# The shift by the row maximum of four attention heads, in one pass of 32-row strips ahead of the scores

## The chip, the cores and the metric

The kernel runs on one core of a Trainium2 chip. The metric is device time in microseconds (us) of one execution, the median of several runs. TensorE does the matrix products into the eight banks of PSUM, ScalarE (ACT) the exponentials and copies, VectorE (DVE) the maxima and normalisation, GpSimd (POOL) small vector work, SyncE (SP) issues the transfers. Each engine works through its own queue in order; semaphores tie them together.

## What is computed

Two transformer blocks over x of 4 sequences x 512 tokens x 256: causal self-attention (16 heads of 16), cross-attention over a context of 4 x 1024 x 192, a soft mixture of experts; then causal attention, cross-attention, and an inner block of causal attention and a routed mixture of experts. After each comes a layer norm. The part that the change touches is the same in all five attentions:

```python
w = jnp.einsum('bhnd,bhmd->bhnm', q, k) * jax.lax.rsqrt(float(D))
w = jnp.where(mask > 0, w, NEG)          # causal layers only
w = jax.nn.softmax(w, axis=-1)
attn = jnp.einsum('bhnm,bhmd->bhnd', w, v)
```

## The kernel before

Two calls of `stage_attentions` hold the five attentions: the first runs a0 (causal, 512 keys) and c0 (context, 1024 keys), the second a1, c1 and a2. Work goes by **groups** of four heads of one sequence, 16 groups for each attention, 80 in all. A group runs over **key tiles** of 128 keys, four in a causal layer, eight in a context layer. In a causal layer, tile t has only the 512 - 128 t query columns from its diagonal on.

Scores are computed with the keys on the 128 output partitions and the queries in the columns. Queries and keys are split into high and low parts, so that a head takes 64 rows of the contraction, and TensorE holds two heads at a time, one in its upper and one in its lower 64 rows. For softmax the row maximum has to be subtracted first, and the maximum belongs to a query, that is to a column; so it is added by a matmul. The steps for one group n are these:

- **Maximum passes** (`unit`, L1200, events "unit"): scores with the queries on the partitions, for group n + 2 while group n runs. Each pass is a pair of matmuls into two banks, from which VectorE takes the maxima (L1431; with a mask in causal layers, L1427).
- **Chain** (six small VectorE steps) turns a group's maxima into three bf16 parts of minus the maximum, in `shift`: for head m of the group in columns 32 m to 32 m + 2.
- **Shift rows** (`shift_rows`, L1254, event "shift"): four matmuls turn `shift`, and ScalarE copies the result to `shift_T` (L1368). Head m now stands in rows 32 m to 32 m + 2.
- **Scores** (`scores`, events ("scores", n, (t, p)) with p = 0, 1): each event fills two banks, for heads p and 2 + p. A pair of matmuls of keys and queries opens the two sums (L1213, 64 rows each), in causal layers two pairs of mask matmuls follow (L1219), and a pair that multiplies `choose` with `shift_T` closes them (L1223, 64 rows each, of which the constant `choose[:, p, :]` picks three).
- **Exponentials** (`exps`, L1357): ScalarE reads each bank and writes probabilities.
- **Values** (`values`, L1235): eight matmuls in four column strips of 32, summed over the key tiles in a bank of their own. It waits until the last exponentials of its tile are done.
- **Drain** (L1364), **turn** (`turn`, L1245) and normalisation follow when a group is through.

All engines follow one list, written out by `attention_plan`, and each takes the events that concern it in the list's order. For a key tile t of group n this reads: scores (t, 0); maximum passes of group n + 2; values of tile t - 1; in tile 1 also the turn of the outputs of group n - 1 and the loads of group n + 3; in the last tile the shift rows of group n + 1; scores (t, 1); maximum passes; two steps of the chain; and then, spread over the tiles by estimated cost, the **pieces**: projections of a later layer's queries, keys ("split", two ScalarE copies each) and values ("value", one copy), turns of rows, and output projections of an earlier one. A context tile has two maximum passes, one in each half.

Banks are handed out in the same order from a ring of seven (`SHARED_BANKS`; the eighth is that of the values). `wait_bank` makes TensorE wait until the event that had the bank seven places before has been read. The first scores of a group wait for the copy of the shift (L1208).

Of the kernel before, what the change touches and what calls it, by code (L numbers as in the profile page):

```python
# [21 lines left out]
F32R = mybir.dt.float32r  # L22
# [6 lines left out]
P = 128  # L29
# [70 lines left out]
@staged  # L100
def stage_constants(c):

    nc = c.nc
    c.x_tok = c.keep("x_tok", [P, NT, D])
    c.ident = c.keep("ident", [P, P])
    c.ident_bf = c.keep("ident_bf", [P, P], BF16)
    c.pick = c.keep("pick", [P, 2, P], F32R)
    c.choose = c.keep("choose", [P, 2, P], F32R)  # L110
    c.mask_qk = c.keep("mask_qk", [P, SEQ])
    c.mask_kq = c.keep("mask_kq", [P, 2, P], F32R)
    c.eps = c.keep("eps", [P, 1])
    c.x_in = [c.ctx.enter_context(nc.semaphore(f"x_in{b}")) for b in range(BATCH)]
    c.made = c.ctx.enter_context(nc.semaphore("const_made"))
    filled = c.sem("const_filled")
    with (nc.sbuf_tensor("tri_kq", [P, P], BF16) as tri_kq,
          nc.sbuf_tensor("chosen", [P, 2, P], BF16) as chosen, nc.Block() as block):
        @block.sync
        def _(sp):  # L120
            for b in range(BATCH):
                sp.dma_start(c.x_tok[:, b * QT:(b + 1) * QT, :], c.args["x"][b].rearrange("(q p) d -> p q d", p=P)
                             ).then_inc(c.x_in[b], 16)

        @block.gpsimd
        def _(pool):
            for t in (c.ident, c.ident_bf, c.mask_qk, tri_kq):
                pool.memset(t[:, :], 0.0).then_inc(filled, 1)
            pool.memset(chosen[:, :, :], 0.0).then_inc(filled, 1)
            pool.memset(c.eps[:, :], LN_EPS).then_inc(c.made, 1)  # L130
            pool.wait_ge(filled, 5)
            for t in (c.ident, c.ident_bf):
                pool.affine_select(out=t[:, :], in_=t[:, :], compare_op=ALU.not_equal, fill=1.0, base=0,
                                   pattern=[[-1, P]], channel_multiplier=1).then_inc(c.made, 1)
            pool.affine_select(out=c.mask_qk[:, SEQ - P:SEQ], in_=c.mask_qk[:, SEQ - P:SEQ], compare_op=ALU.is_ge, fill=NEG_BIG,
                               base=0, pattern=[[-1, P]], channel_multiplier=1).then_inc(c.made, 1)
            pool.affine_select(out=tri_kq[:, :], in_=tri_kq[:, :], compare_op=ALU.is_ge, fill=NEG_BIG,
                               base=0, pattern=[[1, P]], channel_multiplier=-1).then_inc(c.made, 1)


            for i in range(6):
                if i:
                    pool.wait_ge(filled, 5 + 2 * i)
                for p in range(2):
                    pool.affine_select(out=chosen[:, p, :], in_=chosen[:, p, :], compare_op=ALU.not_equal, fill=1.0,
                                       base=-(64 * (i // 3) + 32 * p + i % 3), pattern=[[0, P]], channel_multiplier=1
                                       ).then_inc(filled, 1)

        @block.vector
        def _(v):  # L150
            v.wait_ge(c.made, 5)
            for dst, src in ((c.pick, c.ident_bf), (c.mask_kq, tri_kq)):
                for own in (slice(0, 64), slice(64, P)):
                    for x in range(2):
                        v.tensor_copy(dst[own, x, :], src[64 * x:64 * x + 64, :]).then_inc(c.made, 1)
            v.wait_ge(filled, 17)
            v.tensor_copy(c.choose[:, :, :], chosen[:, :, :]).then_inc(c.made, 1)
            v.wait_ge(c.made, CONSTANTS)


# [566 lines left out]
def attention_plan(layers, pieces, contexts):  # L727

    slots = [layer for layer in layers for _ in range(BATCH)]
    groups = GROUPS * len(slots)
    plan = []

    def layer_of(n):
        return slots[n // GROUPS]

    def share(stream, done, total):  # L740

        while stream and stream[0][1] * total < done * stream[0][2]:
            plan.append(stream.pop(0)[0])

    def stream_of(events):

        whole, at, out = sum(cost for _, cost in events) or 1, 0, []
        for event, cost in events:
            out.append((event, at, whole))
            at += cost  # L750
        return out

    def body(n):
        units, own = [], [(x, COST.get(x[0], 300)) for x in pieces.get(n, ())]
        if 0 <= n + 2 < groups:
            units = stream_of([(("unit", n + 2, u), 1) for u in range(len(layer_of(n + 2).units))])
        if n < 0:
            plan.extend(x for x, _ in own)
            if n == -1:
                plan.extend([("augment", 0, 0), ("vload", 2, 0)])  # L760
                for k in range(SHIFT_STEPS):
                    plan.append(("chain", 0, k))
                    share(units, k + 1, SHIFT_STEPS)
                plan.append(("shift", 0, 0))
            plan.extend(x[0] for x in units)
            return
        if n == groups:
            last = layer_of(n - 1).key_tiles - 1
            plan.extend([("values", n - 1, last), ("drain", n - 1, 0), ("turn", n - 1, 0)])
            plan.extend(x for x, _ in own)  # L770
            return
        layer, own = layer_of(n), stream_of(own)
        steps = layer.key_tiles
        for t in range(steps):
            plan.append(("scores", n, (t, 0)))
            share(units, 2 * t + 1, 2 * steps)
            if t:
                plan.append(("values", n, t - 1))
            elif n:
                plan.extend([("values", n - 1, layer_of(n - 1).key_tiles - 1), ("drain", n - 1, 0)])  # L780
            if t == 1:
                if n:
                    plan.append(("turn", n - 1, 0))
                if n + 1 < groups:
                    plan.append(("augment", n + 1, 0))
                if n + 3 < groups:
                    plan.append(("vload", n + 3, 0))
                if NB <= n + 3 < groups:
                    plan.append(("load", n + 3, 0))
            if t == steps - 1 and n + 1 < groups:  # L790
                plan.append(("shift", n + 1, 0))
            plan.append(("scores", n, (t, 1)))
            share(units, 2 * t + 2, 2 * steps)
            if n + 1 < groups and t < 3:
                plan.extend([("chain", n + 1, 2 * t), ("chain", n + 1, 2 * t + 1)])
            share(own, t + 1, steps)
        assert not units and not own

    for n in range(-3, groups + 1):
        for event in contexts.get(n, ()):  # L800
            plan.append(event)
        body(n)
    return slots, plan
# [3 lines left out]
def stage_attentions(c, name, layers, pieces, contexts):  # L807
# [47 lines left out]
    with ExitStack() as ctx:  # L855
# [141 lines left out]
        with nc.Block() as block:  # L997
# [192 lines left out]
            def _(pe):  # L1190
# [13 lines left out]
                def scores(event):  # L1204
                    _, n, (t, p) = event
                    layer, r = layer_of(n), n % NB
                    if (t, p) == (0, 0):
                        wait_evacuated(pe, ("shift", n, 0))  # L1208
                    wait_bank(pe, event)
                    q0 = t * P if layer.causal else 0  # L1210
                    for h in range(2):
                        own = slice(64 * h, 64 * h + 64)
                        pe.matmul(bank_of(event, h)[:, q0:SEQ], keys_of(n)[own, p, t * P:(t + 1) * P],  # L1213
                                  qs[r][own, p, q0:SEQ], start=True, stop=False)
                    if layer.causal:
                        for x in range(2):
                            for h in range(2):
                                own = slice(64 * h, 64 * h + 64)
                                pe.matmul(bank_of(event, h)[:, q0:q0 + 64 * (x + 1)], c.pick[own, x, :],  # L1219
                                          c.mask_kq[own, x, 0:64 * (x + 1)], start=False, stop=False)  # L1220
                    for h in range(2):
                        own = slice(64 * h, 64 * h + 64)
                        filled(pe.matmul(bank_of(event, h)[:, q0:SEQ], c.choose[own, p, :],  # L1223
                                         shift_T[n % 2][own, q0:SEQ], start=False, stop=True), event)

                def values(event):
                    _, n, t = event
# [1116 lines left out]
```

## Time and profile before

| what | us |
|---|---|
| median of 3 runs (2954.71 to 2956.67) | 2955.36 |
| the profiled execution | 2954.8 |
| its span, first to last instruction | 2953.1 |
| TensorE busy | 2536.9 (86%) |
| VectorE busy | 1502.1 (51%) |
| ScalarE busy | 1340.6 (45%) |
| GpSimd busy | 456.4 (15%) |

The five attentions take about 1754 us of the span; the two mixtures of experts and their norms take the rest. Matmuls are pipelined, and the durations shown for them overlap: how fast TensorE goes is better read from the starts of successive matmuls than from their durations. In the timeline, neighbouring instructions of one kind are merged into one line with their count, and a bracket shows how long the engine had been idle before and what ended that.

### The profile page before, as it was taken

What the parts mean: (1) busy time and instruction counts of PE and PEld (TensorE: products, weight loads), DVE (VectorE), ACT (ScalarE), POOL (GpSimd) and SP (SyncE); (2) the same over time, 40 slices, a digit from 0 to 9 for tenths busy, and PEclk for the clock granted to TensorE, in tenths of its full rate; (3) what the DMA queues carried; (4) which work ended last, traced back from release to release, by engine and by line L of the source; (5) the groups of instructions that cost most, each with busy time, mean ns of one, the idle gap of its engine ahead of it and who ended that gap; (6) DMA issues with size and microseconds to landing.
All of it is one profiled execution on the core that took longest, in us unless ns stands there. A gap on an engine that the chain in (4) does not pass through costs nothing. (4 is left out here: it accounts for less than half of the span.)

```text
span 2953.1 us, 47417 instructions
## 1 busy us (share of the span) xinstructions
PE 2536.9 (86%) x15793; PEld 1452.1 (49%) x15794; DVE 1502.1 (51%) x4196; ACT 1340.6 (45%) x2886; POOL 456.4 (15%) x719
## 2 busy tenths in 40 slices
PE   6999999999549889997889899898977995399991
PEld 3555544444224456675555544343434654267761
DVE  2555877888044500024544588777735663222224
ACT  3655467766444422111445457565664552022220
POOL 4233211110200000000122212212023001400004
PEclk8999999999969999998899999999998996599996
DMA  6544533321000022114633433232322325501113
GB/s 207 165 138 139 132 87 93 75 59 43 6 12 1 1 91 91 60 47 151 182 105 122 133 97 90 58 92 63 78 68 75 108 66 189 176 31 32 32 32 91
DMA packets 153825, 259.89 MB, mean 88 GB/s; under 512 B 22712, under 2 KB 96704, under 8 KB 149440
## 3 DMA queue, kind: packets, MB, share of 16 engines
q1 hardware_dynamic: 150544, 248.81, 28.8%
q0 software_dynamic: 3072, 8.39, 0.9%
q8 instruction: 120, 1.97, 0.3%
q14 instruction: 89, 0.73, 0.1%
HBM read 180.71 MB, written 81.53 MB: 89 GB/s over the span
## 5 line engine op out<-in xcount | busy, mean ns | idle before, releaser
L1357 ACT ACTIVATE second_p<-psum 128x512 f32<-128x512 f32 (+3 forms) x1024 | 461.9, 522 | 278.9 <-PE psum L1223 275.4
L1357 ACT ACTIVATE first_p<-psum 128x512 f32<-128x512 f32 (+3 forms) x768 | 365.8, 548 | 171.5 <-PE psum L1223 168.5
L1431 DVE TENSOR_REDUCE second_max_parts<-psum 128x1 f32<-128x512 f32 x512 | 321.5, 682 | 67.7 <-PE psum L1200 66.5
L1431 DVE TENSOR_REDUCE first_max_parts<-psum 128x1 f32<-128x512 f32 x512 | 322.2, 682 | 57.4 <-PE psum L1200 55.6
L1427 DVE CUSTOM_DVE_ANT_0 second_masked<-psum,mask_qk 128x384 f32<-128x384 f32 (+3 forms) x512 | 229.2, 488 | 194.5 <-PE psum L1200 169.8
L1213 PE MATMUL psum<-second_q,second_k 64*128 64x512 f32 (+3 forms) x1024 | 226.1, 437 | 42.8 <-DVE second_max_parts L1431 27.1
L1235 PE MATMUL psum<-second_p,second_v_aug 128*32 128x512 f32 (+3 forms) x2048 | 238.6, 538 | 8.4 <-ACT second_p L1357 8.1
L1200 PE MATMUL psum<-second_k,second_q 64*128 64x512 f32 (+3 forms) x1024 | 201.9, 391 | 27.9 <-DMA second_k<-a_k_parts 15.6
L1213 PEld LDWEIGHTS psum<-second_q,second_k 64*128 64x128 f32 x1024 | 98.1, 187 | 231.3 <-issue 84.0
L1223 PE MATMUL psum<-second_shift_T,choose 64*128 64x512 f32 (+3 forms) x1024 | 197.6, 381 | 0.0
L1235 PE MATMUL psum<-first_p,first_v_aug 128*32 128x512 f32 (+3 forms) x1536 | 184.1, 551 | 11.6 <-ACT first_p L1357 11.6
L1427 DVE CUSTOM_DVE_ANT_0 first_masked<-psum,mask_qk 128x128 f32<-128x128 f32 (+3 forms) x256 | 114.5, 488 | 132.4 <-PE psum L1200 115.2
L2035 ACT ACTIVATE routed_rows_kept<-psum,routed_bias 128x128 f32<-128x128 f32 x312 | 84.7, 382 | 212.1 <-PE psum L1976 212.1
L1213 PE MATMUL psum<-first_q,first_k 64*128 64x512 f32 (+3 forms) x768 | 171.5, 443 | 2.4 <-DVE first_max_parts L1431 1.4
L1200 PE MATMUL psum<-first_k,first_q 64*128 64x512 f32 (+3 forms) x768 | 154.1, 401 | 21.1 <-DMA first_k<-a_k_parts 9.9
L1223 PE MATMUL psum<-first_shift_T,choose 64*128 64x512 f32 (+3 forms) x768 | 148.3, 382 | 0.0
L1213 PEld LDWEIGHTS psum<-first_q,first_k 64*128 64x128 f32 x768 | 72.1, 184 | 153.4 <-ACT first_p L1357 72.2
L1200 PEld LDWEIGHTS psum<-second_k,second_q 64*128 64x128 f32 x1024 | 103.7, 193 | 81.7 <-issue 47.5
L1966 PE MATMUL psum<-routed_up,routed_rows_T 128*128 x312 | 143.2, 602 | 0.3 <-issue 0.3
L1985 PE MATMUL psum<-routed_down,routed_rows_kept 128*128 x624 | 141.1, 379 | 0.0
L1219 PE MATMUL psum<-mask_kq,pick 64*128 64x64 f32 (+1 forms) x1536 | 135.9, 255 | 0.0
L1219 PEld LDWEIGHTS psum<-mask_kq,pick 64*128 64x128 f32 x1536 | 133.6, 190 | 4.1
(317 smaller groups left out, 3800.4 us busy)
## 6 DMA issues: line engine op xcount, KB each, us to landing
first_k<-c_k_parts SPq DMA_DIRECT2D x64, 256.0 KB, 4.7
second_q<-a_q_parts SPq DMA_DIRECT2D x128, 128.0 KB, 2.9
second_k<-a_k_parts SPq DMA_DIRECT2D x128, 128.0 KB, 2.9
second_k<-c_k_parts SPq DMA_DIRECT2D x64, 256.0 KB, 4.6
first_q<-a_q_parts SPq DMA_DIRECT2D x64, 128.0 KB, 2.9
first_k<-a_k_parts SPq DMA_DIRECT2D x64, 128.0 KB, 2.9
c_k_parts<-first_held SPq DMA_DIRECT2D x16, 512.0 KB, 3.1
first_q<-c_q_parts SPq DMA_DIRECT2D x64, 128.0 KB, 4.5
```

The source lines that it names most:

```text
L1200: ins = pe.matmul(bank_of(event, h)[:, 0:width], qs[r][own, p, qt * P:(qt + 1) * P], keys_of(n)[own, p, k0:k0 + width], start=True, stop=True)
L1213: pe.matmul(bank_of(event, h)[:, q0:SEQ], keys_of(n)[own, p, t * P:(t + 1) * P], qs[r][own, p, q0:SEQ], start=True, stop=False)
L1219: pe.matmul(bank_of(event, h)[:, q0:q0 + 64 * (x + 1)], c.pick[own, x, :], c.mask_kq[own, x, 0:64 * (x + 1)], start=False, stop=False)
L1223: filled(pe.matmul(bank_of(event, h)[:, q0:SEQ], c.choose[own, p, :], shift_T[n % 2][own, q0:SEQ], start=False, stop=True), event)
L1235: ins = pe.matmul(c.psum[32 * j:32 * j + 32, PV_BANK, q0:SEQ], v_aug[n % 2][:, t, j, :], probs[at % 2][:, j, q0:SEQ], start=t == 0, stop=t ...
L1357: evacuated(act.activation(probs[tile % 2][:, 2 * h + p, q0:SEQ], bank[:, q0:SEQ], ACT.Exp, scale=scale), event)
L1427: evacuated(v.tensor_tensor_reduce(masked[:, done % 2, 0:width], bank[:, 0:width], c.mask_qk[:, SEQ - width:SEQ], 1.0, LEAST, ALU.add, ALU ...
L1431: evacuated(v.reduce_max(max_parts[n % 2][:, h, p, qt, k0 // BANK:k0 // BANK + 1], bank[:, 0:width], axis=AX_X), event)
L1966: ins = pe.matmul(c.psum[:, UP_BANK + h, :], rows_T[r][:, k, :], up[:, bass.ds(e, 1), k, h * BANK:(h + 1) * BANK].rearrange("p o n -> p (o ...
L1985: ins = pe.matmul(c.psum[:, DOWN_BANK + r, 0:D], hidden[r][:, m, :], down[:, bass.ds(e, 1), m, :].rearrange("p o n -> p (o n)"), start=m = ...
L2035: act.activation(hidden[r][:, m, :], c.psum[:, TURN_BANK + m // PER, m % PER * P:(m % PER + 1) * P], ACT.Gelu, bias=bias[:, bass.ds(e * HM ...
```

## The change

The constant `choose` becomes one 128 x 128 tile: the sum of its two halves, so that each of the four strips of 32 rows has ones in its first three rows. In the plan, the two score events of a key tile stand together, ahead of the maximum passes and the values. With the first of the two, TensorE waits for the banks of both, and then multiplies `choose` with `shift_T` in four matmuls of 32 rows, one for each head, which open the sums in four banks. Masks and scores of the two events then add to them, and the pair of scores closes them.

```diff
-    c.choose = c.keep("choose", [P, 2, P], F32R)
+    c.choose = c.keep("choose", [P, P], F32R)
...
-            v.tensor_copy(c.choose[:, :, :], chosen[:, :, :]).then_inc(c.made, 1)
+            v.tensor_tensor(c.choose[:, :], chosen[:, 0, :], chosen[:, 1, :], ALU.add).then_inc(c.made, 1)
...
         for t in range(steps):
-            plan.append(("scores", n, (t, 0)))
+            plan.extend([("scores", n, (t, 0)), ("scores", n, (t, 1))])
             share(units, 2 * t + 1, 2 * steps)
...
             if t == steps - 1 and n + 1 < groups:
                 plan.append(("shift", n + 1, 0))
-            plan.append(("scores", n, (t, 1)))
             share(units, 2 * t + 2, 2 * steps)
...
-                    wait_bank(pe, event)
                     q0 = t * P if layer.causal else 0
-                    for h in range(2):
-                        own = slice(64 * h, 64 * h + 64)
-                        pe.matmul(bank_of(event, h)[:, q0:SEQ], keys_of(n)[own, p, t * P:(t + 1) * P],
-                                  qs[r][own, p, q0:SEQ], start=True, stop=False)
+                    if p == 0:
+                        for half in range(2):
+                            wait_bank(pe, ("scores", n, (t, half)))
+                        for m in range(GH):
+                            own = slice(32 * m, 32 * m + 32)
+                            pe.matmul(bank_of(("scores", n, (t, m % 2)), m // 2)[:, q0:SEQ], c.choose[own, :],
+                                      shift_T[n % 2][own, q0:SEQ], start=True, stop=False)
                     if layer.causal:
...
                     for h in range(2):
                         own = slice(64 * h, 64 * h + 64)
-                        filled(pe.matmul(bank_of(event, h)[:, q0:SEQ], c.choose[own, p, :],
-                                         shift_T[n % 2][own, q0:SEQ], start=False, stop=True), event)
+                        filled(pe.matmul(bank_of(event, h)[:, q0:SEQ], keys_of(n)[own, p, t * P:(t + 1) * P],
+                                         qs[r][own, p, q0:SEQ], start=False, stop=True), event)
```

## Rows read from the trace of the kernel before

**Rows 1.** The page's costliest groups, the shift: busy us, mean ns, idle before.

```profile
L1223 PE MATMUL psum<-second_shift_T,choose 64*128 64x512 f32 (+3 forms) x1024 | 197.6, 381 | 0.0
...
L1223 PE MATMUL psum<-first_shift_T,choose 64*128 64x512 f32 (+3 forms) x768 | 148.3, 382 | 0.0
```

**Rows 2.** Stretch of c0: busy PE, PEld, DVE, ACT, POOL; clock, DMA share, GB/s.

```profile
352.00:786.00 434.00, 410.57 (x2792) 183.81 (x2790) 320.16 (x616) 300.13 (x571) 61.46 (x101) 1.00 0.27 67
```

**Rows 3.** Waits of ScalarE in the same stretch: us in total, times, longest.

```profile
ACT first_p L1357 <- PE psum L1223: 109.6, 108, 2.8
```

**Rows 4.** Timeline of a plain key tile of c0: start us, us, engine, line.

```profile
568.06 0.50 PE L1213 MATMUL psum<-first_q,first_k 64*128 64x512 f32 x2
568.39 0.40 PE L1223 MATMUL psum<-first_shift_T,choose 64*128 64x512 f32 x2
568.63 0.40 PE L1200 MATMUL psum<-first_k,first_q 64*128 64x512 f32 x2
568.83 2.07 ACT L1357 ACTIVATE first_p<-psum 128x512 f32<-128x512 f32 x4 [0.87 <-PE psum L1223]
568.87 0.39 PE L1213 MATMUL psum<-first_q,first_k 64*128 64x512 f32 x2
569.06 2.48 DVE L1431 TENSOR_REDUCE first_max_parts<-psum 128x1 f32<-128x512 f32 x4 [0.46 <-PE psum L1200]
569.10 0.40 PE L1223 MATMUL psum<-first_shift_T,choose 64*128 64x512 f32 x2
...
570.00 1.07 PE L1235 MATMUL psum<-first_p,first_v_aug 128*32 128x512 f32 x8
571.00 0.50 PE L1213 MATMUL psum<-first_q,first_k 64*128 64x512 f32 x2
```

**Rows 5.** Timeline, shift rows and their copies of two successive plain context groups.

```profile
577.32 0.60 ACT L1368 ACTIVATE first_shift_T<-psum 128x512 fp32r<-128x512 f32 x1 [0.54 <-PE psum L1254]
...
601.32 0.40 PE L1254 MATMUL psum<-ident_bf,first_shift 128*128 128x128 bf16 x4
...
601.75 0.60 ACT L1368 ACTIVATE first_shift_T<-psum 128x512 fp32r<-128x512 f32 x1 [0.54 <-PE psum L1254]
```

**Rows 6.** Timeline of c0, a key tile with a projection piece and the next.

```profile
361.88 1.07 PE L1235 MATMUL psum<-first_p,first_v_aug 128*32 128x512 f32 x8
...
363.45 0.39 PE L1200 MATMUL psum<-first_k,first_q 64*128 64x512 f32 x2
...
363.77 1.98 PE L1315 MATMUL psum<-first_ctx_T,first_c_wk 128*128 128x512 f32 x4
...
365.68 0.50 PE L1213 MATMUL psum<-first_q,first_k 64*128 64x512 f32 x2
...
365.79 0.69 ACT L1386 ACTIVATE first_held<-psum,first_c_bk 128x512 fp32r<-128x512 f32 x1 [1.06 <-PE psum L1315]
366.02 0.39 PE L1223 MATMUL psum<-first_shift_T,choose 64*128 64x512 f32 x2
...
366.94 1.08 ACT L1357 ACTIVATE first_p<-psum 128x512 f32<-128x512 f32 x2
...
369.51 1.06 PE L1235 MATMUL psum<-first_p,first_v_aug 128*32 128x512 f32 x8
```

**Rows 7.** Timeline of TensorE, a plain group of a2: start, turn, next start.

```profile
2347.94 0.50 PE L1213 MATMUL psum<-second_q,second_k 64*128 64x512 f32 x2
...
2352.57 0.66 PE L1245 MATMUL psum<-ident,second_o_sum 128*128 128x128 f32 x4
2353.15 0.45 PE L1213 MATMUL psum<-second_q,second_k 64*128 64x384 f32 x2
...
2359.51 0.50 PE L1213 MATMUL psum<-second_q,second_k 64*128 64x512 f32 x2
```

**Rows 8.** Timeline of TensorE, a group of a0 with four products: first and last.

```profile
273.20 0.51 PE L1213 MATMUL psum<-first_q,first_k 64*128 64x512 f32 x2
...
291.57 0.50 PE L1213 MATMUL psum<-first_q,first_k 64*128 64x512 f32 x2
```

## The prediction

> **What bounds the kernel now.** I read the totals first: the shift's two lines of matmuls (L1223) keep TensorE busy for 197.6 and 148.3 us [rows 1]. That is an upper mark of what is touched, not of what can be gained: half of it, 173 us, would come back only if TensorE never waited there. Next, the busy time of one stretch: in c0 TensorE is busy 410.57 of 434.00 us at granted clock 1.00, ScalarE 300.13, VectorE 320.16 [rows 2]. So TensorE is nearly full, but the waits of ScalarE in that stretch show something else beside it: 109.6 us in 108 waits for L1223 [rows 3]. The timeline of a plain key tile of a context layer explains both [rows 4]. Values (L1235) of one tile start at 570.00, the next pair of scores at 571.00, and the period (scores 568.06 to 571.00) is 2.94 us. It is a ring through two engines: values 1.00; scores .33 to the shift (568.06 to 568.39); .44 from the shift's start to the first exponential (568.39 to 568.83); two exponentials 1.08 (at 366.94 [rows 6]) and .09 until values start (569.92 to 570.00). 1.00 + .33 + .44 + 1.08 + .09 = 2.94. TensorE alone would need about 2.61 of it; ScalarE idles .87 [rows 4].
>
> Three prices come out of the same rows. Pairs in one tiling follow each other every .23 to .24 us (568.39, 568.63, 568.87, 569.10 [rows 4]). **A pair whose next matmul has another tiling** costs .32 (363.45 to 363.77, 64 rows to 128 [rows 6]): .09 more. **The first pair after such a change** costs .34 instead of .23 (365.68 to 366.02 [rows 6]; 568.06 to 568.39 [rows 4]), since its weight load isn't hidden: .10 more. The same holds for a first pair behind a wait.
>
> **The change, part by part.** There are 64 key tiles in each of a0, a1, a2 and 128 in each of c0, c1: 448 in 80 groups of four heads.
>
> *Removed:* one pass of L1223 in each tile, .23 at 512 columns, less at the 384, 256 and 128 of causal tiles.
>
> *Added:* two tilings more in each tile. The quad is in 32 rows, maximum passes, masks and scores in 64. No row of before shows 32 rows. Its bounds: nothing, if the engine needs no pause between 32 and 64 rows, and .09 + .10 = .19 each way as between 64 and 128 rows [rows 6]. Less than nothing is excluded, since the pass removed is counted already. I take .19: both are changes of row tiling with 128 columns kept, and every one of the changes seen pays it. Into the quad it is hidden where TensorE waits anyway; out of the quad it lies between the quad and the first scores, always on the path.
>
> The Trainium skill, "TensorEngine Tiling (Array Packing)", section "Key Properties", says that changing the tiling mode, not just the tile, drains TensorE. It gives no price; by it the sum is the one taken here, and the .09 of the row from 64 to 128 rows agrees.
>
> *Moved:* both halves of a tile's scores now stand together, and the quad waits for four of seven banks. A plain context tile takes eight banks, so the last of the four waited for by exponentials is the fourth bank of the tile before. Behind that wait the whole of TensorE's queue stands, the next maximum passes and values too; ScalarE waits for the scores. So the ring becomes: quad .34 + .09; first scores to first exponential .10 + .44; four exponentials 2.07 (568.83 [rows 4]); .09 back to TensorE. Sum 3.13, against 2.94. What fits beside it: second scores .34, maximum pass .23, values with the change before them .09 + 1.00, last pass .10 + .32: with the quad about 2.73, under 3.13, so hidden. VectorE has four reduces, 2.48 us in rows of three tiles of this kind, also under it. The four-bank wait asks for one of the passes' reduces too, done over a microsecond earlier.
>
> Group by group (a group runs eight context or four causal tiles):
>
> *Plain context groups, 14 of 32.* Six tiles of 3.13. The second also holds the turn of the outputs (.58, 2352.57 to 2353.15 [rows 7]): TensorE is then the longer, 2.73 + .58 = 3.31. In the last, the shift of the next group is turned and copied, and the first quad needs that copy: before, a pair of scores and a pass stood between; now one pass. Turn at 2.30 after the quad; the copy (.60 [rows 5]) follows the exponentials, which end at 3.04, so the next quad stands at 3.73. Sum 18.78 + 3.31 + 3.73 = 25.8 against 24.43 between copies [rows 5]: +1.4. I take +1.3 for rounding of steps; together +18.
>
> *Context groups with products, 10.* A projection piece takes 1.91 (363.77 to 365.68) and a pair of tiles 7.63 (361.88 to 369.51) [rows 6]. After: 2.73 + 1.91 = 4.64. For a split piece the tile behind it is later by ScalarE's own copies: they run from .11 to 1.26 after TensorE goes on (365.79 and 366.94 against 365.68), so exponentials begin at 1.26 rather than at .97, and that tile takes 3.42. Pair 8.06, +.43; for a value piece, with one copy, 7.77, +.14. With two to four pieces in a group: about +1.1 each, +11. *Groups with output pieces, 8:* the projection waits for ScalarE's copy before and after alike, and the tile's slack swallows the change: 0.
>
> *Plain causal groups, 14 of 48.* By the same prices on the 38 lines of the group from 2347.94 to 2359.51 (11.57 [rows 7]). First tile, ring: .43 + masks .27 + .43 + 2.07 + .09 = 3.29. Second, TensorE with the turn: 3.30. Third: 2.46. Fourth: the shift's turn at 1.85, .43 to its copy (601.32 to 601.75 [rows 5]), .60, .09: 2.97. Sum 12.0: +.4, together +6. *With four products, 12:* TensorE is full (18.37 over 43 lines, 273.20 to 291.57 [rows 8]); a piece changes the tiling between scores and maximum passes already, so only the way out of the quad is new (.19) and a pass of .05 to .23 goes, with the backlog of weight loads behind masks: 18.2, -.2, together -2. *The other 22:* between, +.1, +2.
>
> Everything else (constants, soft MoE, token MoE) does the same work; the one new VectorE instruction replaces one, once, at the start: nothing, and if its cover went, under a microsecond.
>
> **Sum:** 18 + 11 + 0 + 6 - 2 + 2 = +35 us. The profiled execution took 2954.8 us (2953.1 in its span), .6 under the median of 2955.36. 2954.8 + 35 = **2990 us**.
>
> **Rivals.** *Free change between 32 and 64 rows (faster).* Place: from the quad to the first scores, and from the last pass to the quad. Price: nothing. Then the ring is 2.94 at most (.34 + .44 + 2.07 + .09): a plain context group 24.0, -.4; a causal one 10.8, -.8; with four products -1.0, others about -.9; context groups with products -.4, with outputs -1.2. Sum -6 - 4 - 10 - 11 - 12 - 20 = -63: 2892. It decides against my forecast when a change costs less than about .12 of the .19. For it: no row shows 32 rows. Against it: every other change of tiling pays. The skill's same page, section "Theoretical Speedup", gives a contraction of up to 32 rows up to 4 times against 2 times at 64, which is this rival; its word for it is theoretical, and no run here shows it.
>
> *The quad runs as two pairs (the change doesn't do what it says).* If only two of the four row strips stream together, the removed pass is back, and the changes stay: +.23 in 256 context tiles and about .15 in 192 causal ones, 59 + 29 = 88: 2990 + 88 = 3078. For it: no row has four row strips at once. Against it: values stream in four column strips, eight matmuls in 1.07 [rows 4].
>
> *Slack eats it all.* The long waits for loads and for the norms shield some groups: half of the sum, 2972; it lies inside the forecast's own range.
>
> **Chances.** Forecast .74 (own range 2955 to 3030; a tenth of it falls within or below no change), free change .17, two pairs .08, others .01. What a measurement of this kernel can tell from no change is about 0.2%, 6 us: faster .22, same .06, slower .72. The range goes from the free change, 2890, to the upper end of the forecast, 3035; the two pairs are left out.
>
> **What would show it.** Right: in a plain context tile the first score matmul starts .42 to .45 after the quad with an exposed weight load, four exponentials run without a gap, then about 1.1 idle, period 3.1; the first quad of a group waits for the copy of the shift. The free change would show .34 and .23 there and a period of 2.9; two pairs, quad to scores of .65. Wrong: if VectorE's reduces end the quad's wait, or if TensorE's granted clock fell below 1.00 in c0 for its longer waits.

## The result, and the profile after

The changed kernel takes 3040.52 us (3034.29 to 3044.47, 4 runs) against 2956.02 us for the kernel before, run beside it: a ratio of 1.0285, with a 95% interval of 1.0269 to 1.0302. It is slower by about 85 us. The sign was forecast; the size, +35, was not, and the time lies 5.5 us above the range's upper end.

Where the time went is read from the distances between shift copies, one of which opens each group, so that they bound the five attentions (the ends of c0 and a2, which no copy follows, are set behind their last group). Two views of busy time, by stretch: first the kernel before, then the changed one, in the order a0, c0, a1, c1, a2. Columns: stretch and its length, then busy time (and instructions) of TensorE, its weight loads, VectorE, ScalarE and GpSimd, then the granted clock of TensorE as a share of full speed, the share of the DMA engines, and GB/s.

```profile
60.70:351.30 290.60, 279.23 (x2274) 165.53 (x2274) 172.53 (x664) 160.57 (x369) 82.14 (x119) 0.99 0.49 145
351.30:785.00 433.70, 410.47 (x2792) 184.20 (x2792) 320.86 (x617) 300.67 (x572) 62.15 (x102) 1.00 0.27 68
1406.70:1722.10 315.40, 283.80 (x2242) 168.34 (x2242) 172.45 (x664) 154.57 (x358) 71.94 (x108) 0.93 0.46 132
1722.10:2212.70 490.60, 444.30 (x2898) 199.56 (x2898) 353.23 (x735) 315.35 (x594) 95.44 (x171) 0.96 0.29 77
2212.70:2452.00 239.30, 208.65 (x2028) 130.43 (x2032) 136.71 (x604) 123.15 (x310) 31.32 (x58) 0.96 0.26 77
```

```profile
61.40:361.20 299.80, 288.24 (x2282) 163.51 (x2283) 171.44 (x665) 155.92 (x372) 82.93 (x119) 0.98 0.49 142
361.20:808.90 447.70, 409.14 (x2805) 164.84 (x2806) 325.99 (x618) 295.77 (x572) 61.41 (x101) 1.00 0.26 65
1425.00:1767.60 342.60, 308.79 (x2251) 174.47 (x2252) 171.64 (x665) 151.38 (x361) 72.72 (x108) 0.87 0.42 123
1767.60:2276.40 508.80, 442.45 (x2892) 181.67 (x2892) 357.26 (x734) 308.94 (x594) 94.86 (x170) 0.96 0.28 73
2276.40:2541.70 265.30, 229.06 (x2028) 133.48 (x2028) 137.08 (x602) 120.64 (x310) 31.21 (x58) 0.87 0.23 69
```

The context layers lost 14 us (c0) and 18 us (c1) at an unchanged clock. The causal layers lost 9 (a0), 27 (a1) and 26 us (a2), and in the last two the granted clock fell from .93 and .96 to .87. With 32 + 62 = 94 us lost here and 85 to 87 us in the whole, the rest of the kernel, where nothing is changed, took some 8 us less.

A plain key tile of c0 in the timeline of the changed kernel (start us, us, engine, line; L1214 is the quad, the four matmuls of 32 rows, L1224 the scores, L1199 a maximum pass):

```profile
584.56 0.51 PE L1214 MATMUL psum<-first_shift_T,choose 32*128 32x512 f32 x4 [0.37 <-ACT first_p L1358]
585.00 0.73 PE L1224 MATMUL psum<-first_q,first_k 64*128 64x512 f32 x4
585.57 0.40 PE L1199 MATMUL psum<-first_k,first_q 64*128 64x512 f32 x2
585.59 2.06 ACT L1358 ACTIVATE first_p<-psum 128x512 f32<-128x512 f32 x4 [1.13 <-PE psum L1224]
585.89 1.06 PE L1236 MATMUL psum<-first_p,first_v_aug 128*32 128x512 f32 x8
586.89 0.50 PE L1199 MATMUL psum<-first_k,first_q 64*128 64x512 f32 x2
587.76 0.51 PE L1214 MATMUL psum<-first_shift_T,choose 32*128 32x512 f32 x4 [0.37 <-ACT first_p L1358]
```

It answers to [rows 4], and the ring stands in it as forecast: quad to scores .44, scores to the first exponential .59, four exponentials 2.06, back to the next quad .11, in all 3.20 against 2.94. TensorE waits for the fourth exponential (`<-ACT first_p`), ScalarE for the scores: its gap grew from .87 to 1.13 us. The quad itself does what it says: 32 rows, four matmuls at once. On the page its 1024 matmuls of the second call are busy 125.3 us where the shift had 197.6 [rows 1], but TensorE now waits 78.2 us ahead of them. Before, it waited 42.8 us ahead of the scores that opened a tile, and not at all ahead of the shift (the first line is of the kernel before):

```profile
L1213 PE MATMUL psum<-second_q,second_k 64*128 64x512 f32 (+3 forms) x1024 | 226.1, 437 | 42.8 <-DVE second_max_parts L1431 27.1
...
L1224 PE MATMUL psum<-second_q,second_k 64*128 64x512 f32 (+3 forms) x1024 | 199.7, 427 | 0.0
L1214 PE MATMUL psum<-second_shift_T,choose 32*128 32x512 f32 (+3 forms) x1024 | 125.3, 476 | 78.2 <-ACT second_p L1358 35.9
```

So 72 us of matmul time went from that line, and 35 us came back as waiting in front of it. In the whole nothing was saved: on the two pages TensorE's busy time rose from 2536.9 to 2581.4 us, by the views above in the causal layers alone.

### The profile page after: what moved, and what is told of

Same layout as the page of the kernel before. It is cut to its first block and busy times, and to the rows that moved or that the text cites. A ratio compares the mean times of both kernels' runs of the same rounds, so it can differ in the third digit from the quotient of the medians.

```text
span 3040.1 us, 47184 instructions
## 1 busy us (share of the span) xinstructions
PE 2581.4 (85%) x15793; PEld 1417.0 (47%) x15794; DVE 1508.9 (50%) x4196; ACT 1317.3 (43%) x2886; POOL 456.7 (15%) x719
## 5 line engine op out<-in xcount | busy, mean ns | idle before, releaser
L1358 ACT ACTIVATE second_p<-psum 128x512 f32<-128x512 f32 (+3 forms) x1024 | 447.2, 524 | 320.2 <-PE psum L1224 319.8
L1236 PE MATMUL psum<-second_p,second_v_aug 128*32 128x512 f32 (+3 forms) x2048 | 250.1, 563 | 1.1 <-ACT second_o_sum L1365 1.0
L1199 PE MATMUL psum<-second_k,second_q 64*128 64x512 f32 (+3 forms) x1024 | 220.3, 431 | 16.0 <-DMA second_k<-a_k_parts 14.1
L1224 PE MATMUL psum<-second_q,second_k 64*128 64x512 f32 (+3 forms) x1024 | 199.7, 427 | 0.0
L1214 PE MATMUL psum<-second_shift_T,choose 32*128 32x512 f32 (+3 forms) x1024 | 125.3, 476 | 78.2 <-ACT second_p L1358 35.9
L1199 PE MATMUL psum<-first_k,first_q 64*128 64x512 f32 (+3 forms) x768 | 164.2, 431 | 11.4 <-DMA first_k<-a_k_parts 8.3
L1199 PEld LDWEIGHTS psum<-second_k,second_q 64*128 64x128 f32 x1024 | 104.0, 200 | 148.1 <-DVE second_max_parts L1432 57.2
L1220 PE MATMUL psum<-mask_kq,pick 64*128 64x64 f32 (+1 forms) x1536 | 159.5, 291 | 0.0
L1224 PE MATMUL psum<-first_q,first_k 64*128 64x512 f32 (+3 forms) x768 | 141.4, 419 | 0.0
L1214 PEld LDWEIGHTS psum<-second_shift_T,choose 32*128 32x128 f32 x1024 | 54.1, 192 | 171.4 <-issue 72.4
L1199 PEld LDWEIGHTS psum<-first_k,first_q 64*128 64x128 f32 x768 | 73.1, 189 | 120.6 <-DVE first_max_parts L1432 64.2
L1647 DVE TENSOR_TENSOR soft_slots_T<-psum,soft_experts_down_bias 128x256 f32 (+1 forms) x32 | 13.6, 425 | 231.9 <-PE psum L1623 231.9
```

The costliest lines, as they stand in the source:

```text
L1199: ins = pe.matmul(bank_of(event, h)[:, 0:width], qs[r][own, p, qt * P:(qt + 1) * P], keys_of(n)[own, p, k0:k0 + width], start=True, stop=True)
L1214: pe.matmul(bank_of(("scores", n, (t, m % 2)), m // 2)[:, q0:SEQ], c.choose[own, :], shift_T[n % 2][own, q0:SEQ], start=True, stop=False)
L1224: filled(pe.matmul(bank_of(event, h)[:, q0:SEQ], keys_of(n)[own, p, t * P:(t + 1) * P], qs[r][own, p, q0:SEQ], start=False, stop=True), event)
L1236: ins = pe.matmul(c.psum[32 * j:32 * j + 32, PV_BANK, q0:SEQ], v_aug[n % 2][:, t, j, :], probs[at % 2][:, j, q0:SEQ], start=t == 0, stop=t ...
L1358: evacuated(act.activation(probs[tile % 2][:, 2 * h + p, q0:SEQ], bank[:, q0:SEQ], ACT.Exp, scale=scale), event)
```

## Experiments

**The order alone.** The scores of a tile stand together, the shift stays last and in 64 rows:

```diff
-            plan.append(("scores", n, (t, 0)))
+            plan.extend([("scores", n, (t, 0)), ("scores", n, (t, 1))])
...
-            plan.append(("scores", n, (t, 1)))
```

> Only the plan's order is changed: both score events of a key tile stand together; the shift stays in two pairs of 64 rows that close the sums, and each event waits for its own two banks. Theory A (the loss is the ring through four banks: the quad waits for the fourth exponential of the tile before): here the first scores wait for the third exponential only and nothing stands between them and their own exponentials but one pair, so a plain context tile is bound by TensorE at 2.6 to 2.7 us against 2.94 before and 3.19 after; the whole 2900 to 2945 us. Theory B (the order itself costs, since the maximum passes and values now stand behind both events): a plain context tile stays at 3.1 or more and the whole is above 3000 us.

Measured: 2913.56 us, ratio .9853 (.9837 to .9869): faster than before. The order, with two banks waited for at a time, is no part of the loss; it is a gain by itself. Timeline of a plain context tile (here L1212 are scores, L1222 the shift):

```profile
560.07 0.39 PE L1212 MATMUL psum<-first_q,first_k 64*128 64x512 f32 x2
560.29 0.39 PE L1222 MATMUL psum<-first_shift_T,choose 64*128 64x512 f32 x2
...
560.78 2.07 ACT L1356 ACTIVATE first_p<-psum 128x512 f32<-128x512 f32 x4 [0.83 <-PE psum L1222]
561.44 1.06 PE L1234 MATMUL psum<-first_p,first_v_aug 128*32 128x512 f32 x8
562.77 0.39 PE L1212 MATMUL psum<-first_q,first_k 64*128 64x512 f32 x2
```

The period is 2.70 (560.07 to 562.77), and no bracket stands at a TensorE line: values find their exponentials done, and the engine goes from one product to the next.

**Pairs first.** The changed kernel with the quad replaced by two pairs in 64 rows; the order and the wait for four banks are kept:

```diff
-                        for m in range(GH):
-                            own = slice(32 * m, 32 * m + 32)
-                            pe.matmul(bank_of(("scores", n, (t, m % 2)), m // 2)[:, q0:SEQ], c.choose[own, :],
-                                      shift_T[n % 2][own, q0:SEQ], start=True, stop=False)
+                        for half in range(2):
+                            for h in range(2):
+                                own = slice(64 * h, 64 * h + 64)
+                                pe.matmul(bank_of(("scores", n, (t, half)), h)[:, q0:SEQ], c.choose[own, half, :],
+                                          shift_T[n % 2][own, q0:SEQ], start=True, stop=False)
```

> The changed kernel, but its shift goes first in two pairs of 64 rows in place of one quad of 32: order and four-bank wait are kept, no tiling of 32 rows is left. Theory A (wait for four banks; the quad's own price is about its gain): a plain context tile goes from 3.19 to between 3.1 and 3.25, since .23 for the second pair stands against about .2 for the change of tiling; the whole 3010 to 3045 us. Theory C (the tiling of 32 rows is the price): the tile falls to 2.9 to 3.0 and the whole to 2970 or less.

Measured: 2994.96 us, ratio 1.0134 (1.0117 to 1.0151). The time of the whole is neither theory's. Its plain context tile, though, is that of the changed kernel (L1215 the pairs of the shift, L1225 the scores):

```profile
579.44 2.06 ACT L1359 ACTIVATE first_p<-psum 128x512 f32<-128x512 f32 x4 [1.12 <-PE psum L1225]
581.61 0.72 PE L1215 MATMUL psum<-first_shift_T,choose 64*128 64x512 f32 x4 [0.33 <-ACT first_p L1359]
582.14 0.65 PE L1225 MATMUL psum<-first_q,first_k 64*128 64x512 f32 x4
582.62 1.58 ACT L1359 ACTIVATE first_p<-psum 128x512 f32<-128x512 f32 x3 [1.11 <-PE psum L1225]
```

First exponential to first exponential 3.18 (579.44 to 582.62), against 3.20: shift to scores .53 for .44, and scores to exponentials .48 for .59. In the context layers the quad is worth its price and no more, as theory A has it: between shift copies a plain group takes 25.99 us here and 26.13 in the changed kernel. So the 45 us between this kernel and the changed one must lie in the causal layers. In the views by stretch a1 and a2 of this kernel take 322 and 245 us, at a clock of .93 and .96, against 342.6 and 265.3 at .87:

```profile
1422.00:1744.00 322.00, 286.26 (x2250) 173.07 (x2252) 170.92 (x665) 151.14 (x361) 72.90 (x108) 0.93 0.44 130
2252.00:2497.00 245.00, 205.81 (x2031) 131.31 (x2029) 135.63 (x604) 120.67 (x310) 31.29 (x58) 0.96 0.25 75
```

**Own banks.** The kernel with pairs first, except that each event waits for its own two banks only and has its pair of the shift right ahead of its scores:

```diff
-                    if p == 0:
-                        for half in range(2):
-                            wait_bank(pe, ("scores", n, (t, half)))
-                        for half in range(2):
-                            ...
+                    wait_bank(pe, event)
+                    for h in range(2):
+                        own = slice(64 * h, 64 * h + 64)
+                        pe.matmul(bank_of(event, h)[:, q0:SEQ], c.choose[own, p, :],
+                                  shift_T[n % 2][own, q0:SEQ], start=True, stop=False)
```

> The shift first in pairs of 64 rows and the two score events together, as in the kernel with pairs first, but each event waits for its own two banks and has its own pair of the shift right ahead of its scores; nothing else differs. Theory A (the wait for four banks makes the ring of 3.19): a plain context tile falls to about 2.7 us as in the order alone, and the whole to 2905 to 2930 us. Rival (it is the place of the shift, ahead of the scores): the tile stays above 3.0 and the whole above 2970 us.

Measured: 2911.96 us, ratio .9849 (.9832 to .9867). The same products as in the kernel with pairs first, in nearly the same order, are 83 us faster. In the timeline (L1212 the shift, L1222 the scores) the period is 2.71 (561.26 to 563.97):

```profile
561.26 0.40 PE L1212 MATMUL psum<-first_shift_T,choose 64*128 64x512 f32 x2
561.49 0.39 PE L1222 MATMUL psum<-first_q,first_k 64*128 64x512 f32 x2
561.72 0.40 PE L1212 MATMUL psum<-first_shift_T,choose 64*128 64x512 f32 x2
561.98 2.07 ACT L1356 ACTIVATE first_p<-psum 128x512 f32<-128x512 f32 x4 [0.81 <-PE psum L1222]
563.97 0.39 PE L1212 MATMUL psum<-first_shift_T,choose 64*128 64x512 f32 x2
```

To put the shift ahead of the scores costs nothing (2911.96 against 2913.56 with the order alone). What costs is to have four banks free, and both pairs of the shift done, ahead of the first scores: .47 us in each plain context tile (3.18 against 2.71). Pairs first joins the two. By these rows the four-bank wait with only one pair, .23 less, ahead of the first scores would give about 2.95; that is an estimate, and no run tried it.

**The context layers alone, and the causal layers alone.** The plan and the order of the matmuls are those of the changed kernel in the one kind of layer and those of before in the other (`together` is true for the one kind; the constant is that of before, and the quad reads of it the half that it needs). The first kernel's edit stands here; the second has `layer.causal` in its first line:

```diff
+                    together = not layer.causal
+                    if not together:
+                        wait_bank(pe, event)
+                        ...
+                    elif p == 0:
```

> The change in the context layers c0 and c1 alone; causal layers run as before. Theory A: plain context tiles 3.19 as in the changed kernel; by the distances between shift copies c0 and c1 hold about 31 of the 85 us, so 2980 to 2995 us.

> The change in the causal layers a0, a1, a2 alone; context layers run as before. Theory D (in the causal layers of the second call TensorE falls to its lower clock level for longer, since it waits more often): 3005 to 3020 us, with more time at 1.2 GHz in a1 and a2 than before, and groups of 13 to 19 us beside others of 12.3 for the same instructions. Without the clock (waits and tilings alone) the causal layers would cost 48 groups at .4 to .8, so 2975 to 2990 us.

Measured: 2977.92 us for the context layers (ratio 1.0079, 1.0062 to 1.0095), two us under the expected band, and 3019.07 us for the causal layers (1.0214, 1.0194 to 1.0234), within theory D's. Against the 2956.26 of before beside them that is 22 and 63 us, and their sum is the whole loss of 85. In the first, c0 and c1 lost as much as in the changed kernel (14 and 19 us), while a1 and the stretch between c0 and a1 took 4 and 6 us less than before. In the second the clock of a1 and a2 stands at .85, as the view by stretch shows:

```profile
1406.00:1743.00 337.00, 302.63 (x2199) 171.41 (x2198) 174.70 (x702) 146.85 (x348) 70.15 (x106) 0.85 0.43 126
2232.00:2503.00 271.00, 237.03 (x1988) 136.57 (x1980) 140.18 (x614) 121.84 (x304) 31.20 (x58) 0.85 0.23 71
```

**Passes twice.** That the clock costs the time, and isn't only found beside it, asks for a kernel in which nothing but work is added. Plain causal groups of the changed kernel differ in a telling way. Four of a2 by stretch, with the same instructions:

```profile
2362.22:2374.57 12.35, 10.96 (x124) 6.38 (x124) 8.73 (x40) 6.79 (x18) 0.73 (x1) 1.00 0.41 117
2405.42:2424.88 19.46, 18.36 (x122) 10.28 (x122) 8.82 (x40) 6.92 (x19) 0.73 (x1) 0.55 0.20 61
2457.67:2470.01 12.34, 10.99 (x124) 6.41 (x122) 8.73 (x40) 6.79 (x18) 0.73 (x1) 1.00 0.34 96
2469.98:2489.31 19.33, 18.23 (x124) 10.18 (x123) 8.83 (x40) 6.92 (x18) 0.73 (x1) 0.56 0.21 63
```

Two run at the full 2.4 GHz and take 12.3 us; two run almost wholly at 1.2 GHz (.55 and .56) and take 19.4. Before, plain groups of a2 took 11.57 [rows 7]. The experiment multiplies each maximum pass that runs beside such groups twice into the same banks:

```diff
+                    twice = layer.causal and not pieces.get(n - 2)
+                    for again in range(2 if twice else 1):
                         for h in range(2):
...
-                        filled(ins, event)
+                            if again == twice:
+                                filled(ins, event)
```

> The changed kernel with work added and nothing else: in the causal groups that hold no pieces, each maximum pass is multiplied twice into the same banks (1.07 us more of streaming in a group, against .53 that the change took out). Theory D (the lower clock in plain causal groups is what the change loses there): time at 1.2 GHz in a1 and a2 falls from 160 us to 60 to 110, the plain groups of 14 to 19 us fall to 12.3 to 13, and the whole falls to 3000 to 3025 us although work was added. Rival (the causal layers lose by waits and tilings alone): the whole rises to 3045 to 3055 us.

Measured: 3023.86 us, ratio 1.0234 (1.0217 to 1.0251): 17 us less than the changed kernel, with more to do. A plain group of a2 and the second group of a1, then a1 and a2 whole:

```profile
2397.06:2410.23 13.17, 12.23 (x140) 7.42 (x140) 8.78 (x42) 6.79 (x19) 0.73 (x1) 1.00 0.31 91
1442.21:1460.55 18.34, 16.93 (x136) 8.52 (x136) 8.77 (x41) 10.25 (x25) 4.09 (x4) 1.00 0.68 190
```

```profile
1425.00:1755.00 330.00, 299.81 (x2332) 171.93 (x2332) 172.41 (x666) 151.08 (x361) 72.83 (x108) 0.92 0.44 128
2264.00:2519.00 255.00, 221.71 (x2156) 132.94 (x2156) 137.27 (x602) 119.72 (x309) 31.31 (x58) 0.95 0.24 72
```

The plain group takes 13.2 us at the full clock, as all of its kind in a2 do: .8 above the fast ones of the changed kernel for the work added, and a little above the 13 expected. a1 and a2 come to .92 and .95. From 342.6 + 265.3 to 330 + 255 that is 23 us less in spite of 13 groups (209 matmuls more in the two views, 16 a group) x .8 = 10 us more. So the lower clock had cost a1 and a2 some 33 us. Theory D holds, and the rival (3045 to 3055) falls. As a price of the change the 33 us are rough: 6 of them lie in the second group of a1, which took 24.7 us in the changed kernel, but 25.2 before as well, at .79 and .80; and two plain groups of a1 still ran at .79 here, in 16.1 and 16.0 us.

**Values last.** The kernel before with one move: values behind both halves of the next tile.

```diff
-            if t:
-                plan.append(("values", n, t - 1))
-            elif n:
-                ...
...
             plan.append(("scores", n, (t, 1)))
             share(units, 2 * t + 2, 2 * steps)
+            if t:
+                plan.append(("values", n, t - 1))
+            elif n:
+                ...
```

> The kernel before with one move: the values of tile t - 1 (and the drain) stand behind both halves of tile t, no longer between them. Theory A (before, a plain context tile was a ring through values, one pair of scores and two exponentials): values find their exponentials done long before, and the tile is bound by TensorE at 2.6 to 2.7 us; the whole 2905 to 2930 us. If 2.94 was the engine's own limit, no change.

Measured: 2968.8 us, ratio 1.0044 (1.0029 to 1.0058): slower, and a miss. The plain context tile takes 2.99 (583.45 to 586.44). Its timeline shows why (L1213 scores, L1200 a maximum pass, L1235 values):

```profile
583.45 0.51 PE L1213 MATMUL psum<-first_q,first_k 64*128 64x512 f32 x2
584.28 2.07 ACT L1357 ACTIVATE first_p<-psum 128x512 f32<-128x512 f32 x4 [0.93 <-PE psum L1223]
585.02 0.49 PE L1200 MATMUL psum<-first_k,first_q 64*128 64x512 f32 x2 [0.15 <-ACT first_p L1357]
585.45 1.06 PE L1235 MATMUL psum<-first_p,first_v_aug 128*32 128x512 f32 x8
586.44 0.51 PE L1213 MATMUL psum<-first_q,first_k 64*128 64x512 f32 x2
```

The second maximum pass waits for the first exponential of its own tile: a tile takes eight banks of a ring of seven, so the eighth is the tile's own first. The values no longer wait for exponentials, but the pass ahead of them does. So the run makes a new ring and doesn't test my account of the old one, through the values; I had not looked at which bank is next.

**Shift early.** The order alone, with the turn of the next group's shift ahead of the values, in context layers one tile earlier:

```diff
+            if t == max(3, steps - 2) and n + 1 < groups:
+                plan.append(("shift", n + 1, 0))
             if t:
                 plan.append(("values", n, t - 1))
...
-            if t == steps - 1 and n + 1 < groups:
-                plan.append(("shift", n + 1, 0))
```

> The order alone, and the turn of the next group's shift moved ahead of the values, in context layers one tile earlier too. Theory A: in the order alone the last tile of a plain context group takes 3.55 against 2.71 and that of a plain causal group .4 to .5 more than its work, since the first scores wait for the copy of the shift; with the copy behind the values these waits go: 80 groups at .3 to .8, so 2870 to 2895 us.

Measured: 2905.19 us, ratio .9823 (.9807 to .9839), 1.8% under the kernel before beside it and the fastest of all. It gained 8 us on the order alone, not 20 or more, a miss: by the distances between shift copies a plain group of a2 takes 11.13 us for 11.27, and a plain context group is no shorter (23.2 to 23.6 for 23.17 in c0). Why so little of the waits came back was not taken apart.

## Why the prediction was right, and where it failed

*The ring.* Right. Forecast 3.13 for a plain context tile, measured 3.20. The changes of tiling cost between 32 and 64 rows what the rows of before showed between 64 and 128: quad to scores .44 for a forecast .43, and .34 from the first pair of scores to the second, as forecast. The Trainium skill, "TensorEngine Tiling (Array Packing)", "Key Properties", has every change of mode drain the engine; this trace agrees, with .44 from the quad to the scores, where behind the same wait a pair in the tiling of the scores is followed after .30 (pairs first: .53 over two pairs, of which the second takes .23). The .43 was right in its sum, less so in its parts: .34 behind a wait and .09 for the change were forecast, .30 and .14 are what these two kernels show. The rivals of the free change and of two pairs are out by the same .44 (.34 and .65 were their marks). Of the .07 missing, .05 lies between scores and first exponential, .59 for .54. The first exponential of a tile carries one more wait than the others (for values, L1354 in the code of before), and where it ended a gap it began .48 to .49 after its matmul in the kernels with the order alone, with pairs first and with own banks (560.29 to 560.78, 582.14 to 582.62, 561.49 to 561.98), against .44 for an exponential without it [rows 4]. That the wait is the cause was not tried.

*The context layers* were forecast at 18 + 11 + 0 = +29 us. The stretches show +32. The sum came out better than its terms, and there is luck in that. Between shift copies most plain groups lost 1.7 us and not 1.3 (24.43 to 26.13), but the last but one of c0 got 4.7 us shorter, so that the fourteen lost 16. The ten with products lost 10. The eight with output pieces, put at 0 because slack would swallow the change, lost .7 to .8 each (29.93 to 30.67 for most), 6 in all.

*The causal layers* were forecast at 6 - 2 + 2 = +6, and measured at +62. This step failed, in two terms.

The first is a cost that the sum did not hold. I named the clock among the things that would make me wrong, but only for c0, where it stayed at 1.00, and priced nothing for a1 and a2, where the kernel before already stood at .93 and .96. By passes twice some 33 of the 56 us missed are that, or 27 without the group of a1 that was as slow before. Pairs first gives a like figure by another way: at the clock of before, a1 and a2 lost 12 us in it; the quad in place of two pairs added .3 us to a plain group at the full clock (12.05 to 12.33 between shift copies) and .1 to one with outputs (18.37 to 18.49), by estimate 6 us in 32 groups; of the 53 us that a1 and a2 lost, 35 are left for the clock.

The second is that the causal groups cost more at the full clock as well. Plain groups went from 11.57 to 12.35, not to 12.0. The group with four products of [rows 8] was forecast at 18.2 and took 18.71 (279.14 to 297.85). It shows a wait that I had not counted: the piece of its first tile (L1316) waits .16 us for a bank, which an exponential has to free first:

```profile
279.14 0.50 PE L1214 MATMUL psum<-first_shift_T,choose 32*128 32x512 f32 x4 [0.26 <-ACT first_shift_T L1369]
...
280.39 2.06 ACT L1358 ACTIVATE first_p<-psum 128x512 f32<-128x512 f32 x4 [1.30 <-PE psum L1224]
...
281.62 1.95 PE L1316 MATMUL psum<-first_ctx_T,first_c_wk 128*128 128x512 f32 x4 [0.16 <-ACT first_p L1358]
...
297.85 0.51 PE L1214 MATMUL psum<-first_shift_T,choose 32*128 32x512 f32 x4
```

a0 lost 9 us in 16 groups, and the clock had a part in it too: 5.8 us lie in its first and its last group, where it stood at .71 for .85 and at .93 for 1.00. The fourteen groups between ran at 1.00 in both kernels and lost 3.4 us (the kernel before first):

```profile
76.92:328.29 251.37, 242.28 (x2000) 144.51 (x2001) 144.61 (x590) 139.73 (x324) 71.12 (x106) 1.00 0.47 142
81.15:335.95 254.80, 246.11 (x2000) 140.72 (x2000) 143.07 (x590) 135.40 (x323) 70.76 (x106) 1.00 0.46 137
```

So the 62 us are some 27 to 35 of the clock in a1 and a2, 18 to 26 beside it there, .6 to .8 a group, and 9 in a0. How the .6 to .8 divides between such waits, the tilings and the weight loads behind the masks was not taken apart.

*The four-bank wait.* I took it for the price of the ring and forecast its length rightly, but did not ask what the order would give without it. Own banks answers: 83 us against pairs first. The change joined a gain (the order, -43) to two losses, the four-bank wait and the clock.

## What to carry to other kernels

Before asking for several banks at once, write down which use of each bank must end first: in a ring of seven with eight banks a tile, the fourth bank's reader, not the matmuls saved, set the pace. The pass saved on an engine that waits in a ring bought nothing; an order that lets the engine take the next product without waiting bought 1.5% here with every product kept. Where the granted clock of a stretch is already below full, price a change there at both clock levels: here the kernel with work added to such stretches was the faster by 17 us.

## What the runs showed of the hardware

Two plain causal groups with equal instructions took 12.3 and 19.4 us, the one at a granted clock of 1.00, the other at .55. What went before the fall at 2405.42, in the changed kernel by stretch: a group with outputs, then a plain group, both at the full clock, with TensorE busy for 16.0 of 18.4 and 11.1 of 12.4 us.

```profile
2374.57:2393.00 18.43, 16.03 (x148) 10.03 (x146) 10.13 (x42) 7.88 (x20) 0.73 (x1) 1.00 0.21 66
2393.00:2405.42 12.42, 11.07 (x126) 6.49 (x126) 8.73 (x40) 6.79 (x19) 0.73 (x1) 1.00 0.32 96
```

The busy share doesn't tell these groups from those that hold the clock: a plain group of a2 with pairs first is busy 10.60 of 12.00 us, and its a2 stands at .96 against .87. In the matmuls the two kernels differ by the quad against two pairs. Why the clock falls with the one and not with the other stays open.
